# Octets of the scan in pairs, with the products that read z made as 64x64 quarters of the array

## The reference, cut to what matters

```
Abar = sigmoid(A)                                  # 512 channels x 16 states
def step(h, xt):                                   # xt: one token of z
    h = h * Abar + xt[..., None] * B_ssm
    y = einsum('bcs,cs->bc', h, C_ssm) + D_ssm * xt
    return (h, y)
_, ys = lax.scan(step, h0, swapaxes(z, 0, 1))
```

## Time and profile before

| | |
|---|---|
| time, median of 3 runs | 2051.77 us (2051.49 to 2053.08) |
| profiled execution: time, span | 2050.9 us, 2049.1 us |
| TensorE's mean granted clock | 0.999 |
| PE busy | 2034.8 us, 99% of the span |
| DVE, ACT, POOL busy | 1435.1, 1094.5, 772.5 us |
| the scan on TensorE | 369.25 us to about 537 us |
| DMA in 369 to 537 us | 0.80 busy, 253 GB/s |

### The profile page before, as it was taken

The page is one execution under the profiler, slowest core; times in us unless marked ns, Lnnn a source line. Parts: engine busy times, 40 slices in busy tenths (PEclk is TensorE's granted clock), DMA queues, the critical chain, the costliest instruction groups (busy, mean ns, idle before and its releaser), DMA issues.

```text
span 2049.1 us, 27189 instructions
## 1 busy us (share of the span) xinstructions
PE 2034.8 (99%) x8987; PEld 1615.0 (79%) x8987; DVE 1435.1 (70%) x2869; ACT 1094.5 (53%) x1843; POOL 772.5 (38%) x778
## 2 busy tenths in 40 slices
PE   9999999999999999999999999999999999999998
PEld 6887888544588888888888888888888888888887
DVE  6998875656666666666666775677767767777776
ACT  4555555323355555555555556655555555555553
POOL 1001111344434444443444443244444444444444
PEclk9999999999999999999999999999999999999999
DMA  5766663887544443443544443322222222222211
GB/s 200 258 212 220 197 217 126 274 266 220 187 133 142 133 143 121 137 138 120 160 125 130 144 129 123 134 73 73 73 93 87 78 90 86 72 72 72 73 42 42
DMA packets 215476, 277.35 MB, mean 135 GB/s; under 512 B 47784, under 2 KB 146344, under 8 KB 212776
## 3 DMA queue, kind: packets, MB, share of 16 engines
q1 hardware_dynamic: 202072, 251.83, 38.0%
q10 hardware_dynamic: 13264, 23.79, 3.3%
HBM read 169.53 MB, written 101.83 MB: 132 GB/s over the span
## 4 chain that ended last, share of the span: by engine, by line
PE 93%; DVE 2%; DMA 2%; ACT 2%; issue 1%; POOL 1%; SPq 0%; ACTq 0%; POOLq 0%; DVEq 0%
PE bank L105 24%; PE bank L106 24%; PE bank L107 24%; PE bank L1562 8%; PE bank L2106 3%; PE bank L914 3%; PE bank L939 3%; PE bank L936 3%; PE bank L1524 1%; DMA bv_row<-in_L_attn_bv 0%; DMA b_w_raw<-in_L_attn_w_w 0%; PE bank L1578 0%; DVE e_w_lo L1933 0%; DMA d_v<-scr_v 0%; DMA d_qx<-d_qb 0%
## 5 line engine op out<-in xcount | busy, mean ns | idle before, releaser
L105 PE MATMUL bank<-e_ring,e_w_hi 128*128 128x512 f32 x512 | 200.7, 392 | 0.0
L106 PE MATMUL bank<-e_ring,e_w_hi 128*128 128x512 f32 x512 | 199.3, 389 | 0.0
L107 PE MATMUL bank<-e_ring,e_w_lo 128*128 128x512 f32 x512 | 199.2, 389 | 0.0
L1562 PE MATMUL bank<-d_kh,d_nat 128*128 128x512 f32 x768 | 192.0, 399 | 0.0
L1826 POOL TENSOR_TENSOR e_x<-e_x,e_beta 128x512 f32<-128x512 f32 x64 | 91.4, 1448 | 217.7 <-ACT e_y L1869 217.7
L1880 ACT ACTIVATE e_kr<-bank 128x512 f32<-128x512 f32 x64 | 38.0, 594 | 243.7 <-PE bank L107 243.7
L1562 PEld LDWEIGHTS bank<-d_kh,d_nat 128*128 128x128 f32 x768 | 139.7, 188 | 27.7
L1951 DVE TENSOR_TENSOR e_ring<-e_mixed,e_ring 128x512 fp32r<-128x512 f32 x128 | 93.5, 731 | 88.0 <-ACT e_ring L1844 88.0
L1808 POOL TENSOR_TENSOR e_x<-e_x,e_ff 128x512 f32<-128x512 f32 x64 | 83.3, 1302 | 175.4 <-DVE e_ff L2017 175.4
L1439 DVE TENSOR_TENSOR d_nat<-d_xn,d_nat 128x512 fp32r<-128x512 f32 x64 | 63.8, 997 | 102.1 <-ACT d_nat L1297 102.1
L1183 POOL TENSOR_TENSOR d_kacc<-d_kacc,d_kr 128x512 f32<-128x512 f32 x64 | 82.7, 1292 | 137.9 <-ACT d_kr L1270 137.9
(11 more groups left out here) (215 smaller groups left out, 6109.7 us busy)
## 6 DMA issues: line engine op xcount, KB each, us to landing
scr_v<-b_vt SPq DMA_DIRECT2D x64, 256.0 KB, 2.7
scr_z<-b_zt SPq DMA_DIRECT2D x64, 256.0 KB, 2.1
c_z<-scr_z SPq DMA_DIRECT2D x64, 256.0 KB, 4.5
scr_y<-c_y ACTq DMA_DIRECT2D x64, 256.0 KB, 4.0
d_x<-in_L_attn_x SPq DMA_DIRECT2D x64, 256.0 KB, 5.4
d_v<-scr_v SPq DMA_DIRECT2D x32, 512.0 KB, 5.8
scr_x<-d_x SPq DMA_DIRECT2D x64, 256.0 KB, 2.8
scr_xnt<-d_xt SPq DMA_DIRECT2D x32, 512.0 KB, 4.3
```

What stands on the lines that cost most here:

```text
L105: eng.matmul(out, lhs[hi], rhs[hi], start=first, stop=False, skip_group_check=onto)
L106: eng.matmul(out, lhs[hi], rhs[lo], start=False, stop=False, skip_group_check=onto)
L107: return eng.matmul(out, lhs[lo], rhs[hi], start=False, stop=last, skip_group_check=onto)
L1562: mm = pe.matmul(BG[c][:, :], s[:, i, cols], r[:, j, :], start=M % NTB == 0 and i == j, stop=M % NTB == NTB - 1 and i == 1, skip_group_che ...
```

## The change

Octets go in pairs p = (2p, 2p+1). The channels of a pair are ordered so that partitions 0 to 63 of one state or y tile hold the first half (i = 0 or 1) of octet 2p and partitions 64 to 127 the same half of octet 2p+1; `abc`, `d_rows`, the short kernel in HBM and the store of y follow that order. z stays in the old order.

The tables `into` and `toep` shrink from 128x128 to 128x64 (a block diagonal of four channels in each half of the partitions); `outof` stays 128x128. own(p) and within(p) are four products of 64x64 by 64x512 each, on the four quarters of the array: rows i of the partitions, columns k (the octet of the pair), into bank[i]. All four of own(p) count on `own_full`, and DVE waits for all. The order on TensorE is own(p+1), within(p), out_of(2p), out_of(2p+1). SB now has four banks and FB two, with `turn_weight` at octets 24, 26, 28 and 30. TABS is 6.

```diff
             if g == 8:
                 sp.wait_ge(k_step, 3)
-                sp.dma_start(scr["kern"].rearrange("o c x -> c o x"), kpad[:, :, :]).then_inc(kern_out, 16)
+                k = scr["kern"]
+                for h in range(2):
+                    for i in range(2):
+                        to = bass.AP(k.tensor, (h * OCTET + i * OCTET // 2) * 2 * CHUNK,
+                                     [[2 * CHUNK, OCTET // 2], [2 * OCTET * 2 * CHUNK, NO // 2], [1, 2 * CHUNK]])
+                        sp.dma_start(to, kpad[h * OCTET // 2:(h + 1) * OCTET // 2, i:NO:2, :]).then_inc(kern_out, 16)
...
-    Z, Y, TABS = 6, 4, 3
+    Z, Y, TABS = 6, 4, 6
+    HALF = P // 2
+    EIGHTHS = OCTET // 2
...
-    FB, YB, SB = banks[0:4], banks[4:6], banks[6:8]
+    FB, YB, SB = banks[2:4], banks[4:6], (banks[6:8], banks[0:2])
...
-    y_of = scr["y"].rearrange("(o c) m n -> o (c m) n", c=OCTET)
-    TURN_AT, WEIGHTS_AT, QUANTISE_AT = 24, 32, 7
+    y_of = scr["y"].rearrange("(p k i e) m n -> p i k (e m) n", k=2, i=2, e=EIGHTHS)
+    mask4 = keep["mask4"]
+    TURN_AT, WEIGHTS_AT, QUANTISE_AT = {24: 0, 26: 1, 28: 2, 30: 3}, 32, 7
...
-            sp.wait_ge(y_full, o - Z + 1)
+            sp.wait_ge(y_full, (o - Z) // 2 * 2 + 1)
             load_z(o)
...
-            for tile, rows in ((into[i], into_t[:, o, :]), (toep[i], toep_t[:, o, :]),
-                               (outof[i], out_pow[:, o, 1:CHUNK + 1])):
-                nc.gpsimd.tensor_tensor(tile[:, :, :], rows.unsqueeze(1).broadcast_to([P, OCTET, CHUNK]), blocks,
+            for tile, rows in ((into[i], into_t[:, o, :]), (toep[i], toep_t[:, o, :])):
+                nc.gpsimd.tensor_tensor(tile[:, :, :], rows.unsqueeze(1).broadcast_to([P, EIGHTHS, CHUNK]), half_blocks,
                                         ALU.mult).then_inc(tab_done, 1)
+            nc.gpsimd.tensor_tensor(outof[i][:, :, :],
+                                    out_pow[:, o, 1:CHUNK + 1].unsqueeze(1).broadcast_to([P, OCTET, CHUNK]), blocks,
+                                    ALU.mult).then_inc(tab_done, 1)
...
         def scan(o):
-            dve.wait_ge(own_full, o + 1)
+            dve.wait_ge(own_full, 4 * (o // 2 + 1))
...
     def tensor(pe):
-        def own(o):
-            pe.wait_ge(z_in[o % Z], 16 * (o // Z + 1))
-            pe.wait_ge(tab_done, 3 * (o + 1))
-            if o >= 2:
-                pe.wait_ge(state_done, B * (o - 1))
-            pe.matmul(SB[o % 2][:, :], into[o % TABS][:, :, :].rearrange("p c s -> p (c s)"), zo[o % Z][:, :],
-                      start=True, stop=True).then_inc(own_full, 1)
+        def quarters(bank, tables, p, stop):
+            for i, k in ((0, 0), (1, 1), (0, 1), (1, 0)):
+                o, rows = 2 * p + k, slice(i * HALF, (i + 1) * HALF)
+                yield pe.matmul(bank[i][k * HALF:(k + 1) * HALF, :],
+                                tables[o % TABS][rows, :, :].rearrange("p e s -> p (e s)"), zo[o % Z][rows, :],
+                                start=True, stop=stop, skip_group_check=not stop)
+
+        def own(p):
+            for o in (2 * p, 2 * p + 1):
+                pe.wait_ge(z_in[o % Z], 16 * (o // Z + 1))
+            pe.wait_ge(tab_done, 3 * (2 * p + 2))
+            if p >= 2:
+                pe.wait_ge(state_done, B * (2 * p - 2))
+            for mm in quarters(SB[p % 2], into, p, True):
+                mm.then_inc(own_full, 1)
+
+        def within(p):
+            if p:
+                pe.wait_ge(y_done, 2 * p)
+            for mm in quarters(YB, toep, p, False):
+                pass
+
+        def out_of(t):
+            pe.wait_ge(state_done, B * (t + 1))
+            pe.matmul(YB[t % 2][:, :], outof[t % TABS][:, :, :].rearrange("p c m -> p (c m)"),
+                      state[t % 2][:, :, :].rearrange("p b n -> p (b n)"), start=False, stop=True,
+                      skip_group_check=True).then_inc(y_full, 1)
...
             if kt == 0:
                 pe.wait_ge(q_step, len(QUANTISE_STEPS))
+            if kt >= 2:
+                pe.wait_ge(w_lo, KT + kt - 1)
...
         own(0)
         pe.wait_ge(*project["v_taken"])
-        for o in range(NO):
...
+        for p in range(NO // 2):
+            if p + 1 < NO // 2:
+                own(p + 1)
+            within(p)
+            for o in (2 * p, 2 * p + 1):
+                out_of(o)
+                if o in TURN_AT:
+                    turn_weight(TURN_AT[o])
+                if o == MIX_BANKS_AT:
+                    mix["open_banks"]()
```

More of the change, by code:

```diff
@@ L303, in sync @@
                 sp.wait_ge(k_step, 3)
-                sp.dma_start(scr["kern"].rearrange("o c x -> c o x"), kpad[:, :, :]).then_inc(kern_out, 16)
+                k = scr["kern"]
[4 more added lines that the diff above has]
+                        sp.dma_start(to, kpad[h * OCTET // 2:(h + 1) * OCTET // 2, i:NO:2, :]).then_inc(kern_out, 16)
             if g == 9:
-                sp.wait_ge(kern_out, 16)
+                sp.wait_ge(kern_out, 4 * 16)
                 k = scr["kern"]
@@ L677, in phase_scan @@
     state = [tokens.tile(f"c_state{i}", [P, B, NCB]) for i in range(2)]
-    into = [tokens.tile(f"c_into{i}", [P, OCTET, NS]) for i in range(TABS)]
-    toep = [tokens.tile(f"c_toep{i}", [P, OCTET, CHUNK]) for i in range(TABS)]
+    into = [tokens.tile(f"c_into{i}", [P, EIGHTHS, NS]) for i in range(TABS)]
+    toep = [tokens.tile(f"c_toep{i}", [P, EIGHTHS, CHUNK]) for i in range(TABS)]
     outof = [tokens.tile(f"c_outof{i}", [P, OCTET, CHUNK]) for i in range(TABS)]
@@ L760, in gpsimd @@
         blocks = mask8.unsqueeze(2).broadcast_to([P, OCTET, CHUNK])
+        half_blocks = mask4.unsqueeze(2).broadcast_to([P, EIGHTHS, CHUNK])
         for o in range(NO):
@@ L784, in scan @@
             for b in range(B):
-                nc.vector.tensor_tensor_scan(state[o % 2][:, b, 1:], rate, SB[o % 2][:, b * NCB:(b + 1) * NCB - 1],
+                nc.vector.tensor_tensor_scan(state[o % 2][:, b, 1:], rate, SB[o // 2 % 2][o % 2][:, b * NCB:(b + 1) * NCB - 1],
                                              0.0, ALU.mult, ALU.add).then_inc(state_done, 1)
@@ L831, in vector @@
                 quantise_step(o - QUANTISE_AT)
-            if TURN_AT <= o - 2 < TURN_AT + KT:
-                kt = o - 2 - TURN_AT
+            if o - 2 in TURN_AT:
+                kt = TURN_AT[o - 2]
                 dve.wait_ge(f_hi, kt + 1)
-                nc.vector.tensor_tensor(wf[:, 1, kt, :], FB[kt][:, :], wf[:, 0, kt, :].bitcast(F32), ALU.subtract)\
+                nc.vector.tensor_tensor(wf[:, 1, kt, :], FB[kt % 2][:, :], wf[:, 0, kt, :].bitcast(F32), ALU.subtract)\
                   .then_inc(w_lo, 1)
@@ L857, in store @@
             act.wait_ge(y_done, o + 1)
-            act.dma_start(y_of[o], yo[o % Y][:, :]).then_inc(y_stored[o % Y], 16)
+            act.dma_start(y_of[o // 2, o % 2], yo[o % Y][:, :]).then_inc(y_stored[o % Y], 16)
         def weight_high(i, kt, tile, raw):
@@ L883, in scalar @@
                 mix["load_bias"]((o - BIASES_AT) // 2)
-            if TURN_AT <= o - 1 < TURN_AT + KT:
-                kt = o - 1 - TURN_AT
+            if o - 1 in TURN_AT:
+                kt = TURN_AT[o - 1]
                 act.wait_ge(f_turned, kt + 1)
-                nc.scalar.activation(wf[:, 0, kt, :], FB[kt][:, :], ACT.Copy).then_inc(f_hi, 1)
+                nc.scalar.activation(wf[:, 0, kt, :], FB[kt % 2][:, :], ACT.Copy).then_inc(f_hi, 1)
             if WEIGHTS_AT <= o < WEIGHTS_AT + 2 * KT:
@@ L923, in turn_weight @@
                 pe.wait_ge(q_step, len(QUANTISE_STEPS))
+            if kt >= 2:
+                pe.wait_ge(w_lo, KT + kt - 1)
             for ot in range(KT):
-                mm = pe.transpose(FB[kt][:, ot * P:(ot + 1) * P], wf_nat[:, pairs_of(ot, kt)],
+                mm = pe.transpose(FB[kt % 2][:, ot * P:(ot + 1) * P], wf_nat[:, pairs_of(ot, kt)],
                                   ident[:, :])
@@ L2222, in two_layer_kernel @@
     keep["bv_row"] = mem.tile("bv_row", [P, D])
-    keep["consts"] = mem.tile("consts", [P, P + 16])
+    keep["consts"] = mem.tile("consts", [P, P + 20])
     after_ident = mem.at
@@ L2233, in two_layer_kernel @@
     keep["bits"] = keep["consts"][:, P + OCTET:P + 16]
+    keep["mask4"] = keep["consts"][:, P + 16:P + 20]
     keep["col"] = {name: keep["cols"][:, i * KT:(i + 1) * KT]
@@ L2285, in per_partition, with by_state @@
         return a.reshape(KT, P, -1).transpose(1, 0, 2).reshape(P, -1)
-    def by_octet(a):
-        return a.reshape(OCT, OCTET, NS).transpose(1, 2, 0).reshape(P, OCT)
+    def by_state(a):
+        return a.reshape(OCT // 2, 2, 2, OCTET // 2, -1).transpose(1, 3, 4, 0, 2).reshape(-1, OCT)
     laid = {name: a for name, a in raw.items() if name not in PACKED}
@@ L2297 @@
     laid["a_rows"] = np.repeat(rows[:, None], CHUNK, axis=1).reshape(P, OCT * NS)
-    laid["abc"] = np.stack([by_octet(raw[n]) for n in ("L0_attn_A", "L0_attn_B_ssm", "L0_attn_C_ssm")], axis=1)
-    laid["d_rows"] = raw["L0_attn_D_ssm"].reshape(OCT, OCTET).T
```

(5 more changed lines are left out.)

## The result

The changed kernel takes 2283.45 us (2279.89 to 2284.28, 4 runs) against 2052.43 before: 1.112 times as long, 95% interval 1.110 to 1.114. The forecast was 2038, the range 2018 to 2082. Of the kernels further down, e4 had one execution of ten at 2140.06 us and e11 one of four at 2894.28 us, both at a lower granted clock (0.90 and 0.65); their times here are those of the others. The span grows from 2049.1 to 2281.4 us, by 232.3.

The account below looks back on a forecast made before the run. TensorE, full throughout the scan, was taken as the bound, with z's loads setting the new pace. 31 pairs x (5.15 - 4.46) = 21.4 us, less 1.0, 1.5, 4.5 and 1.0, gave 13.4 us gained: 2038 us, range 2018 to 2082.

Parts of the forecast that it names:

- Nothing is charged for the following: Costs taken as zero in the scan: POOL's tables, ACT's takes, the short kernel's three extra DMA issues, turning the weight.
- the traffic comes out alike: Scan's DMA: 287 GB/s against 311 before, without the weight piece 240 against 241, so earlier landing times may be used.
- The products: Scan on TensorE: a set of four quarters takes 0.86 us, plus 0.3 stagger; TensorE's own cycle 4.13 us a pair.
- Rival A: Quarters' records start strictly in program order, 430 ns apart; 5.98 us a pair, 2078 us; chance 0.22.
- rival C: Quarters run one after another on TensorE; 3.8 us more a pair, 2170 us; chance 0.08.
- The changes between quarters and full array: TensorE's switch of array mode, twice a pair: 0.2 us each taken, up to 0.35 if the array empties first.
- The loop of z: Scan's z loads, issued too late for own(p), set the pace: 4.46 us a pair, above TensorE's own 4.13.
- rival B: z lands later, second landing 6.0 us, T = 4.9, give-backs eat the gain: 2050 us; chance 0.12.
- the prediction's own formula: Period of a pair in z's loop: T = (L + 3.07) / 2, L from issue until own may start, mean 5.85 us.
- 1 us, between 0 and 3: Give-back for preparing the mix's first tiles, whose DMA round trips have SP's z loads queued behind their waits.
- the splitting of weights: Octets 32 to 39, ACT and DVE: about 5.6 us a pair, 4 pairs x 1.1 = 4.5 us given back.
- Quantising: Octets 7 to 13, on DVE beside the scans: 4.9 us a pair for 4.46, 1.5 us given back.

Follow-up runs that it names:

- e4: Changed kernel with the store of y back in the old pattern, 128 rows in one piece: 2052.20 us, ratio 0.9999 to the kernel before.
- e11: e7 with both stores of y of a pair issued behind the pair's second copy: 2034.54 us, ratio 0.9898.
- e2: Kernel before with only the store of y in the new pattern (2 x 64 rows): 2276.87 us, one run.
- e1: Changed kernel with each store of y issued as two stores of 64 rows: 2059.5 us, ratio 1.0030 to the kernel before.
- e5: e1 with eight buffers for z in place of six, each pair's loads issued one pair earlier: 2046.73 us, ratio 0.9964.
- e7: e6 with the mix's first loads issued behind the last load of z: 2030.04 us, ratio 0.9890.
- e6: Changed kernel, pair order moved to z, loaded in two halves on SP; y stored in one plain piece, eight z buffers: 2041.59 us, ratio 0.9948.

## Why the prediction was wrong

**The step that failed** is one that the prediction did not make. Under "Nothing is charged for the following" stand the three extra issues for the short kernel, POOL and the copies; the store of y, whose address pattern the diff changes in one line, has no term at all. It enters once, where "the traffic comes out alike: four transfers of 256 KB and a weight piece": the same bytes, so the same transfer. Measured, the store runs at 49 to 53 GB/s, its issues hold ACT for 4.3 us in the median, and a pair takes 11.7 us for the 4.46 forecast. e2 shows that this one line is worth 224 us, e1 that without it the rest costs 7.

**What waits:** I had named the right place for a late copy ("take(2p+1) ends ... behind which own lies") and judged it covered because ACT idled 111.1 us. That idle time is a sum over the stage; within a pair the second copy has only own's 0.86 us of cover, and an issue that stands in the same queue goes straight through it. In the changed kernel within waits 5.4 to 9.0 us for it in each pair between 400 and 480 us, in e5 still 0.64 a pair.

**The products: right.** A set of four quarters ran in 0.86 us with 0.07 of stagger, where 0.3 was taken. Rival A expected a stair of 430 ns (0.43 x 4 + 0.43, some 2.2 us for the set) and rival C 3.4: 1.09 us refutes both. The changes between quarters and full array: in e11 own to within is 0.90 us, within to outof 0.97, two outofs to own 1.92 (two slots of 0.86 and 0.20), so 0.04, 0.11 and 0.20 above the slots, 3.79 a pair for the 4.13 taken. In e7 it is 3.89 (0.10, 0.16 and 0.19), with within held for ACT's copy. So a change of mode, taken at 0.2, costs 0.1 to 0.2, less than the 0.35 that a full drain was priced at.

**The loop of z: right in kind, mis-sized.** It was there with six buffers: e5 shows 12.8 us for it. e1 and e4 came out at 5.1 us a pair instead of 4.46. In e4, where ACT issues one plain store, the term that was too small is the landing of a pair's second load, taken at 5.4 us early on: the median of nine pairs issued in 390 to 434 us is 6.17. All loads of that stretch of e4, both of each pair:

```profile
L731 SPq DMA_DIRECT2D c_z<-scr_z x18: 319/376/455, 392.7 to 432.4; - x18
...
DMA to landing us min/median/max: 4.6/5.7/7.2
```

By the prediction's own formula that gives 4.95 us a pair, and own(5) to own(14) took 4.93; that is the case of rival B (a second landing of 6.0, T = 4.9, 2050 us). Between 434 and 450 us, among the loads of x, second landings reach 9.0. For e1 I had not added the copies' loop, nor a doubled issue; and load_front between the loads of octets 60 and 61 (6.9 us of waiting in e4, 7.8 in e6) was in the code that I read, under "1 us, between 0 and 3". The start cost more as well: the two outofs ahead of own(2), forecast to end at about 376.9, end when own(2) starts, at 379.4 in e1 and 379.7 in e4 (381.8 in e7).

**DVE: right in kind.** In the splitting of weights the pairs do get longer, but the four of own(18) to own(22) take 5.0 us each in e1 and in e7 (20.0 and 20.2 in all), between 4.2 and 5.8, for the 5.6 forecast. The terms listed for the 5.6 add up to 6.3. Against e7's undisturbed 3.89 the four cost 4.6 us, and 4.5 was charged, which is partly luck. Quantising cost less than forecast: e7's pairs of own(5) to own(9) take 4.2 us each, for 4.9. The prediction gave DVE a quarter of room; by the earlier trace rows it was 38% (104.3 of 168 us busy).

**The sum:** with the store mended (e1, +0.3%; e4, none) the forecast of -13.4 us would still have been wrong; the gain in the order of the forecast, and then beyond it, came only with the buffers, the plain store and the order of SP's queue (e7, -22 us). That e7's mean pair of 4.43 us lies so near the 4.46 forecast is chance: z's loop no longer sets it, its undisturbed pairs take 3.89, and the rest are single waits.

## What to carry to other kernels

When a diff changes an address pattern, price that transfer anew: the same bytes in the same rows are not the same transfer if the pattern's outermost dimension is small (here no cost that shows at 16 and 8, 3% at 4, 11% at 2); let the engine issue two plain pieces, or move the reordering to the side whose queue is idle. Idle time of an engine over a stage says nothing about the cover of one instruction in it; follow the two or three that stand between a bank's last product and its next. And a stage that is made faster by a quarter needs its prefetch distances, counted in octets, checked in microseconds, with every large transfer that some other stage has put into the same queue.

## What the runs showed of the hardware

Products with two records each (float32) ran four side by side on the quarters: a set took 1.09 us for a full product's 1.02, with the four first records starting together and the four second ones 0.48 us later. In which order the program holds the records the trace doesn't say, so it refutes rival A's stair, not its premise. A store with an outermost dimension of 2 kept two packets under way and moved 49 to 53 GB/s. A DMA issue can hold its engine for up to 10.6 us when the transfers before it are slow, 20 times its usual 0.5 (0.33 for a plain one), and other transfers' issues pay behind it (L892, 7.20 us; the same load's issue in e5 takes 0.35). TensorE's granted clock was 0.67 to 0.69 in a stage with gaps of 5.4 to 9.0 us, and behind a single gap of 7.8 us in e6 the next records ran at half speed (1.98 us for 1.09).
